# Up blocks that begin with the other PSUM bank, and four moves in the queues of VectorE, ScalarE and POOL

## The reference, cut to what matters

```
ln  = layernorm(layernorm(x));   xn = layernorm(ctx)         # with gains and offsets
q   = ln @ W_q;   k, v = split(concat(xn @ W_kv, ln @ W_kv)) # 4 heads of 64
sim = rmsnorm(q) * gq / 8  .  rmsnorm(k) * gk                # 256 x 333 per head, masked
x   = x + softmax(sim) @ v @ W_out + b_out
x2  = layernorm(x)
w   = router(x2 @ gate)    # sigmoid, best group of 4, best 2 of 8 experts, weights x 2.5
x   = x + sum_e w_e * relu(x2 @ up_e)^2 @ down_e + relu(x2 @ up_s)^2 @ down_s
```

## Time and profile before

| what | us |
|---|---|
| median of 3 runs (lowest to highest) | 1199.18 (1198.08 to 1201.65) |
| the profiled execution's own time | 1199.88 |
| its span, first to last instruction | 1198.1 |
| VectorE busy, share | 1021.4, 85% |
| ScalarE busy, share | 790.8, 66% |
| POOL busy, share | 547.9, 46% |

### The profile page before, as it was taken

One profiled execution on the slowest core, in us unless ns is written; L12 is line 12 of the kernel. 1 busy time (PEld: TensorE's weight loads), 2 busy tenths in 40 slices (PEclk: granted clock), 3 DMA queues, 4 the chain that ended last, 5 costly groups with the idle time before them and its releaser, 6 DMA issues.

```text
span 1198.1 us, 32986 instructions
## 1 busy us (share of the span) xinstructions
PE 1158.1 (97%) x11772; PEld 1073.1 (90%) x11772; DVE 1021.4 (85%) x3500; ACT 790.8 (66%) x1900; POOL 547.9 (46%) x473
## 2 busy tenths in 40 slices
PE   7799999999999999999999999999999999999997
PEld 6699999999989999999999999999999999999997
DVE  6689888888988888888889888899888898888876
ACT  5567766667766667666767666667666677666673
POOL 5444445445445345444345444444454444454442
PEclk9899999999999999999999999999999999999999
DMA  5000000000000000000000000000000000000000
GB/s 181 2 13 22 23 22 22 2 22 22 22 22 22 2 23 22 23 22 23 2 22 23 22 22 12 12 22 23 22 23 10 13 23 22 23 22 5 8 10 18
DMA packets 28145, 26.06 MB, mean 22 GB/s; under 512 B 6544, under 2 KB 27440, under 8 KB 27984
## 3 DMA queue, kind: packets, MB, share of 16 engines
q1 hardware_dynamic: 27904, 23.83, 6.4%
q0 software_dynamic: 80, 0.14, 0.1%
HBM read 15.57 MB, written 8.39 MB: 20 GB/s over the span
## 4 chain that ended last, share of the span: by engine, by line
PE 56%; DVE 18%; ACT 13%; issue 11%; ACTq 1%; DMA 0%; DVEq 0%; POOL 0%; SPq 0%
PE attn_ps L411 7%; ACT probs L676 6%; PE up_ps L295 5%; PE up_ps L297 5%; PE up_ps L296 5%; PE attn_ps L397 5%; PE down_ps L295 5%; PE down_ps L297 4%; PE down_ps L296 4%; PE attn_ps L295 4%; PE attn_ps L297 4%; PE attn_ps L296 4%; DVE acc L1065 3%; ACT relu_sb L721 3%; DVE k_lo L892 2%
## 5 line engine op out<-in xcount | busy, mean ns | idle before, releaser
L1262 POOL TENSOR_TENSOR hid_lo<-relu,hid_hi 128x512 fp32r<-128x512 f32 x192 | 247.2, 1288 | 268.3 <-DVE hid_hi L1050 158.0
L1065 DVE SCALAR_TENSOR_TENSOR acc<-down_ps,route_w,acc 128x256 f32<-128x256 f32 x512 | 222.0, 475 | 15.9 <-PE down_ps L297 15.3
L295 PE MATMUL down_ps<-down_hi,hid_hi 128*128 128x256 f32 x768 | 234.0, 305 | 1.4 <-ACT hid_hi L726 0.8
L295 PE MATMUL up_ps<-x_hi,up_hi 128*128 128x256 f32 x768 | 225.9, 294 | 7.9 <-DVE x_lo L974 7.7
L297 PE MATMUL down_ps<-down_hi,hid_lo 128*128 128x256 f32 x768 | 216.6, 282 | 0.0
L296 PE MATMUL down_ps<-down_lo,hid_hi 128*128 128x256 f32 x768 | 216.3, 282 | 0.0
L296 PE MATMUL up_ps<-x_lo,up_hi 128*128 128x256 f32 x768 | 214.4, 279 | 0.0
L297 PE MATMUL up_ps<-x_hi,up_lo 128*128 128x256 f32 x768 | 214.4, 279 | 0.0
L676 ACT ACTIVATE probs<-masked,neg_max,q_scale 128x333 f32<-128x333 f32 x256 | 168.5, 659 | 68.3 <-DVE neg_max L911 68.3
L295 PEld LDWEIGHTS up_ps<-x_hi,up_hi 128*128 128x128 f32 x768 | 144.5, 188 | 16.1 <-issue 9.8
L295 PEld LDWEIGHTS down_ps<-down_hi,hid_hi 128*128 128x128 f32 x768 | 145.1, 189 | 13.9 <-issue 12.8
(11 more groups left out here) (145 smaller groups left out, 2856.9 us busy)
## 6 DMA issues: line engine op xcount, KB each, us to landing
out<-acc SPq DMA_DIRECT2D x31, 256.0 KB, 2.2
x_first<-in_x SPq DMA_DIRECT2D x16, 256.0 KB, 2.7
w_stage<-in_x SPq DMA_DIRECT2D x16, 256.0 KB, 2.8
up_stage<-in_up_t SPq DMA_DIRECT2D x1, 1536.0 KB, 7.5
down_stage<-in_down_t SPq DMA_DIRECT2D x1, 1536.0 KB, 8.6
c_first<-in_ctx SPq DMA_DIRECT2D x16, 77.0 KB
w_stage<-in_ctx SPq DMA_DIRECT2D x16, 77.0 KB
w_stage<-in_w_kv SPq DMA_DIRECT2D x1, 512.0 KB, 5.4
```

What stands on the lines that cost most here:

```text
L295: nc.tensor.matmul(out_ap, s_hi, m_hi, start=first, stop=False)
L1065: nc.vector.scalar_tensor_tensor(acc[:, t, :], down_ps[:, (e + 1) % 2, t * D:(t + 1) * D], route_w[:, t, e:e + 1], acc[:, t, :], ALU.mult, ...
L1262: nc.gpsimd.tensor_tensor(hid_lo[:, p % HID_RING, :], relu2[:, p % 2, :], hid_hi[:, p % HID_RING, :], ALU.subtract).then_inc(hid_lo_done, 1)
```

## The change

It has five parts, and no instruction is added or taken away:

- Banks: in `up` the pairs use the other bank (the first pair bank 1, the second bank 0). The halves of `transpose_ln` and `spread_inverse` change bank with them, and ScalarE's reads.
- The wait for q's low part goes from the first to the second `up` block, and VectorE subtracts x2's low part ahead of q's.
- The variance (L827, L828) is a function of its own, `variance1`, and from step 1 on it stands behind the first `negate_max`.
- ScalarE does pair 2 of `hidden` ahead of the softmaxes of heads 0 and 1.
- POOL does the residual and `rstd_first` behind pair 2 of `hidden_low`: now pairs 0, 1, 2, then `rstd_first`, `residual`, pairs 3 and 4. Before it was `residual`, pair 0, `rstd_first`, pairs 1 to 4.

```diff
@@ transpose_ln (PE); ln_full (ACT) reads the same bank
-    nc.tensor.transpose(up_ps[:, ft, t * P:(t + 1) * P], x_hat[:, t, ft * P:(ft + 1) * P], ident[:])
+    nc.tensor.transpose(up_ps[:, 1 - ft, t * P:(t + 1) * P], x_hat[:, t, ft * P:(ft + 1) * P], ident[:])
@@ spread_inverse (PE); inverse_out (ACT) reads the same bank
-    last = nc.tensor.transpose(up_ps[:, 0, ft * S + t * P:ft * S + (t + 1) * P],
+    last = nc.tensor.transpose(up_ps[:, 1, ft * S + t * P:ft * S + (t + 1) * P],
@@ up (PE)
     if p == 0:
         pe.wait_ge(x2_hi_done, (b + 1) * FT)
         pe.wait_ge(x2_lo_done, (b + 1) * FT)
-        if following:
-            pe.wait_ge(q_lo_done, b + 2)
+    if p == 1 and following:
+        pe.wait_ge(q_lo_done, b + 2)
...
-    last = split_product(up_ps[:, p % 2, j * S:(j + 1) * S], ...
+    last = split_product(up_ps[:, (p + 1) % 2, j * S:(j + 1) * S], ...
@@ hidden (ACT)
-    nc.scalar.activation(relu_sb[:, p % 2, :], up_ps[:, p % 2, :], ACT.Relu).then_inc(relu_done, 1)
+    nc.scalar.activation(relu_sb[:, p % 2, :], up_ps[:, (p + 1) % 2, :], ACT.Relu).then_inc(relu_done, 1)
@@ step (ACT)
     ffn(1)
+    ffn(2)
     softmax(b, 0, first)
     softmax(b, 1, first)
-    ffn(2)
     softmax(b, 2, first)
@@ layer_norm1 (DVE)
-    dve.wait_ge(ln1_step, k + LN1_STEPS)
+
+def variance1(b, first):
+    dve.wait_ge(ln1_step, b * LN1_STEPS + LN1_STEPS)
     if not first:
         dve.wait_ge(rstd1_done, b)
     nc.vector.tensor_scalar(var1[:, 0:T], ...
@@ step (DVE); at the start of the kernel variance1 stands right behind layer_norm1
     negate_max(b, 0)
+    if following and not first:
+        variance1(b + 1, False)
...
     k_normalize(b + 1, 1, False)
+    x2_low(b)
     q_low(b + 1)
-    x2_low(b)
     add(6)
@@ step (POOL)
     q_scales(b, first)
-    residual(b, first)
     if first:
         ... (the low parts of the down weights)
     low(0)
+    low(1)
+    low(2)
     if following and not first:
         rstd_first(b + 1, False)
-    for p in range(1, 5):
-        low(p)
+    residual(b, first)
+    low(3)
+    low(4)
```

More of the change, by code:

```diff
@@ L312, in transpose_ln @@
                     for t in range(T):
-                        nc.tensor.transpose(up_ps[:, ft, t * P:(t + 1) * P], x_hat[:, t, ft * P:(ft + 1) * P], ident[:])
-                    nc.tensor.transpose(up_ps[:, ft, S:KEYS], c_hat[:, ft * P:(ft + 1) * P],
+                        nc.tensor.transpose(up_ps[:, 1 - ft, t * P:(t + 1) * P], x_hat[:, t, ft * P:(ft + 1) * P], ident[:])
+                    nc.tensor.transpose(up_ps[:, 1 - ft, S:KEYS], c_hat[:, ft * P:(ft + 1) * P],
                                         ident[0:C, 0:C]).then_inc(lnt_ps, 1)
@@ L483, in up @@
                         cols = slice((2 * p + j) * P, (2 * p + j + 1) * P)
-                        last = split_product(up_ps[:, p % 2, j * S:(j + 1) * S], (up_hi[:, k, cols], up_lo[:, k, cols]),
+                        last = split_product(up_ps[:, (p + 1) % 2, j * S:(j + 1) * S], (up_hi[:, k, cols], up_lo[:, k, cols]),
                                              (x2_hi[:, k, :], x2_lo[:, k, :]), k == 0, k == FT - 1)
@@ L634, in ln_full @@
                     for k, cols in enumerate((slice(0, S), slice(S, KEYS))):
-                        last = nc.scalar.activation(ln_t[:, ft, cols], up_ps[:, ft, cols], ACT.Identity,
+                        last = nc.scalar.activation(ln_t[:, ft, cols], up_ps[:, 1 - ft, cols], ACT.Identity,
                                                     bias=ln_b[:, k, ft:ft + 1], scale=ln_g[:, k, ft:ft + 1])
@@ L689, in inverse_out @@
                     act.wait_ge(attn_done, b)
-                nc.scalar.activation(inv_t[:], up_ps[:, 0, :].rearrange("p (f s) -> p f s", f=FT),
+                nc.scalar.activation(inv_t[:], up_ps[:, 1, :].rearrange("p (f s) -> p f s", f=FT),
                                      ACT.Copy).then_inc(inv_done, 1)
@@ L1176, in _ @@
             layer_norm1(0, True)
+            variance1(0, True)
             normalize1(0, True)
@@ L1191, in _ @@
             layer_norm1(1, False)
+            variance1(1, False)
             k_normalize(0, 0, True)
```

## The result

| | kernel before | changed kernel |
|---|---|---|
| median of the runs | 1199.45 us (4 runs, 1198.08 to 1201.65) | 1172.76 us (4 runs, 1171.52 to 1175.12) |
| ratio, 95% interval | | 0.9773 (0.976 to 0.9786) |
| profiled execution (span) | 1199.88 (1198.1) us | 1171.52 (1169.7) us |

The change brings 26.7 us. The forecast was 1179.1, 20.4 us of gain against this median, and its range ended at 1175: the sign was right, the size too small by a quarter. All times and ratios in this document leave out four executions that were far slower than the rest (5666 us once for start_wait, 1396.7 once for var_only, 2842 twice for the kernel before).

A forecast was written before the change was run, and what follows sets the result against it. TensorE, busy 97% of the span, was taken to bound the kernel. Savings of 12.2, 7.5 and 0.4 us, together 20.1, took the profiled 1199.88 to 1179.8, or 1179.1 us against the median; range 1175 to 1193.

The forecast's parts named there:

- The first `up` block: TensorE's wait for x2's low part at L295, 30 times: taken as 0.25 us each, bounded from 0.19 to 0.32.
- part 1: Bank swaps and x2's low part ahead of q's on VectorE: removes the 0.25 us wait 30 times, 7.5 us.
- The fourth head's transposes: TensorE's wait at L397 for ScalarE's copy out of PSUM, 29 times: 0.42 us each, predicted to go.
- the chain: Earlier VectorE, ScalarE and POOL work up to the fourth transposes: ScalarE's copy ready 0.7 us early instead of 0.42 late.
- the third `up` block: TensorE's block starting at 602.78 instead of 603.02, out 1.69 us later, so ScalarE's relu 2 starts at 604.47.
- Relu, copy and mask 4: ScalarE's relu 3 at 608.75, its copy from 610.42 to 610.89, and VectorE's mask 4 near 608.27.
- One router level: Level 5 (L1004) on VectorE: starts at 606.29, its last part held until POOL's hid_lo ends at 607.66.
- rival (c): POOL's rstd power holds VectorE's port, delaying router levels 6 and 7: slower, 1204 to 1211 us; chance 0.08.
- Rival (b): POOL's residual holds router levels 7 or 8 until 609.74, spending both gains: about 1199 us; chance 0.06.
- Rival (a): k_lo, a POOL result or a maximum is late, so one stall remains: 1187 to 1192 us; chance 0.12.
- the sum: Whole kernel: TensorE's two repeated stalls, 12.2 and 7.5 us, plus 0.4 in the first block, together 20.1 us.
- The first block's term: TensorE's 6.4 us wait for a maximum in the first block: 0.4 gained, bounds 1.3 gained or 0.9 lost.

The follow-up runs named there:

- start_wait: Changed kernel, with GpSimd in the first batch waiting for VectorE's low parts before the wide subtractions of down_lo: 1167.58 us (ratio 0.9729).
- var_only: Kernel before with only the moved variance and GpSimd's new order; old banks, q's low part first, ScalarE's old order: 1196.48 us (ratio 0.9977).
- pair5_first: Kernel before with ScalarE taking pair 5's relu and hidden part ahead of the copies of heads 4 and 5: 1210.63 us (ratio 1.0093).
- no_act: Changed kernel with ScalarE's old order, softmaxes 0 and 1 ahead of pair 2: 1188.16 us (ratio 0.9896).
- banks_act: Kernel before with new banks, x2's low part first and ScalarE's new order, without the variance and GpSimd moves: 1189.32 us (ratio 0.991).
- after_delay: Changed kernel with one more VectorE copy per batch, right behind the first inv_wide: 1174.84 us (ratio 0.9786).
- banks_act_thin: banks_act with expert 0's scaled addition on VectorE narrowed from 256 to 8 columns per half: 1189.55 us (ratio 0.9909).
- banks_x2: Kernel before with only the new banks, q's wait at the second up block and x2's low part first: 1202.10 us (ratio 1.0016).
- pool_old_order: Changed kernel with GpSimd's old order (residual, pair 0, rstd, pairs 1 to 4) behind the moved variance: 1185.76 us (ratio 0.9889).

## Why the prediction was right and wrong

**The first `up` block: right.** 0.25 per batch was forecast; TensorE's starts give 0.27, and taking part 1 out of the full change costs 8 us against 7.5.

**The fourth head's transposes: right as a chain, too small as a price.** 0.49 measured against 0.42 (0.43 up to the first transpose, as forecast; the 0.06 behind it was not counted). In the chain one step was added up wrong, and it did no harm: the third `up` block is out 1.66 later by the terms that are named there, not 1.69. Relu, copy and mask 4 (594.70, so 608.12; forecast 608.27) stand within 0.15 of the clock that was worked out. One router level is held to GpSimd's end (594.30, so 607.72; forecast 607.66), though it is L1010, one level behind the one named. rstd held nothing: rival (c) fell on that row. (The prediction's own evidence against (c), a k_norm with one source, was of another kind; L1012, L1015 and L1017, with two inputs in SBUF, are the direct test.) Rival (b)'s residual found the levels done, 0.30 after the last of them (594.62 plus 0.15, and 595.07). Rival (a) did not come: no wait for `k_lo` repeats.

**The step that failed is the sum.** "29 x 0.42 = 12.2, and 30 x 0.25 = 7.5 ... Together 20.1" was made from the stalls that the list of waits names, because the prediction held that the list "names them" all: an edit is worth what it does to TensorE's idle moments, "and no more". Two terms are missing. One is the wait of transpose_ln for pair 5's relu, 0.15 x 29 = 4.4 us; its idle time is hidden, because the row's matmul ends are modelled and reach over it, and it shows only in the steps: 0.39 where 0.29 is enough, and 0.17 where 0.11 is enough behind it. pair5_first isolates it. The other is 0.06 x 29 = 1.7 us, the piece of the fourth transposes' stall that lies behind the first of them: the `up` block starts 0.31 after it before and 0.25 after it now. With them and the two sizes as measured (0.27 x 30 = 8.1, 0.43 x 29 = 12.5) the batches give 26.7. The profiled executions differ by 28.4; the remaining 1.7 lie in the first batches and the tail and were not taken apart. The first block's term, 0.4 gained, had the wrong sign: the wait there grew by 0.5, inside the bound of 0.9. The first batch takes 33.9 us where it took 33.3. That the medians of the runs also differ by 26.7 is chance, for the executions in which the steps were measured differ by 28.4.

**A margin that was not looked at, and held.** The prediction asked what is late next for `k_lo`, the maxima and GpSimd's results, and not for the additions. Their cover was 0.37 us against 0.91 of gain. Had VectorE come no sooner, 0.46 per batch would have gone again, as in no_act: 1188. It came right because the forecast's own chain brings VectorE 0.70 forward, but that was not argued: here the forecast was lucky.

**"The parts add up" is false for this change.** Gains in us, each against executions of the kernel before that were made beside it:

| parts present | gain |
|---|---|
| banks and x2 first | -1.8 |
| variance and GpSimd | 3.1 |
| ScalarE's order | 6.5 |
| banks, ScalarE's order | 11.0 |
| banks, variance and GpSimd | 12.2 |
| variance and GpSimd, ScalarE's order | 18.8 |
| all | 26.7 |

The three alone sum to 7.8. Part 1 is worth -1.8 on the kernel before, 4.5 behind ScalarE's order, and 8 to 9 once the variance has moved.

## What to carry to other kernels

Add up the gains per period first, and then hold the sum against the cover of every signal that the gaining engine waits for, also of those that are in no list of waits: cover is the unstalled start less the producer's end less the time of the signal (from VectorE's addition 0.15 us here, from GpSimd's `hid_lo` 0.10, from ScalarE's relu 0.05). Look for hidden stalls in the steps between starts, not in the idle column: the same pair of groups with two different steps (0.39 and 0.29; 0.24 and 0.12 at expert 2's down block in banks_act) is a stall when the longer one ends, batch after batch, at the same distance behind a producer's end. And shorten work ahead of the point to which the other engine is tied; behind it a hold takes back what was gained.

## What the runs showed of the hardware

- A wide subtraction on GpSimd (`hid_lo`, 1.29 us) holds more than VectorE's two-input instructions in SBUF. The copy that widens four reciprocals to 128x256 takes 0.28 us when GpSimd is idle (after_delay), 0.54 when it starts 0.39 before the end of a `hid_lo` (after_delay), and 1.06 when it starts 0.38 after its beginning (banks_act_thin); in both it ends 0.15 after GpSimd's.
- GpSimd's powers (rstd, 0.85 us on 128x3) held none of the router's instructions that ran inside them (L1012, L1015, L1017 of the changed kernel: 0.16, 0.16, 0.15).
- A matmul that waited started 0.15 us after the end of VectorE's addition out of its bank (eight of the kernels), 0.10 after GpSimd's `hid_lo` (banks_act, banks_act_thin, banks_x2, pool_old_order), after ScalarE's copy out of its bank 0.14, but after ScalarE's relu out of its bank 0.05 (both in the kernel before and banks_x2). Why ScalarE's two differ, no run here shows.
- Stalls of 0.13 to 0.20 us were invisible as idle time, and TensorE's busy time fell by 12.4 us with the same 11772 matmuls.
